# Feed-forward four slots behind attention, with its weights staged elsewhere and its two input projections in each other's banks

## What is computed

```
xn  = layernorm(x)
q   = xn @ Wq.T;  lat = xn @ Wkv_down.T;  k = lat @ Wk_up.T;  v = lat @ Wv_up.T
att = softmax(q k^T / 8) v @ Wo.T
xq  = fp4(xn)                        # block scale = max|x| / 6, nearest grid value
h   = silu(xq @ fp4(w_gate).T) * (xq @ fp4(w_up).T)
out = x + att + fp4(h) @ fp4(w_down).T
```

## Time and profile before

| | |
|---|---|
| median of 3 runs | 1498.85 us (1498.58 to 1499.34) |
| profiled execution | 1497.88 us |
| its span, first to last instruction | 1496.1 us |
| mean granted TensorE clock | 0.984 |
| TensorE busy | 1383.9 us (93%) |
| GpSimd busy | 1213.7 us (81%) |
| VectorE busy | 1189.6 us (80%) |
| ScalarE busy | 716.9 us (48%) |

### The profile page before, as it was taken

The page is one execution under the profiler, slowest core; times in us unless marked ns, Lnnn a source line. Parts: engine busy times, 40 slices in busy tenths (PEclk is TensorE's granted clock), DMA queues, the critical chain, the costliest instruction groups (busy, mean ns, idle before and its releaser), DMA issues.

```text
span 1496.1 us, 25492 instructions
## 1 busy us (share of the span) xinstructions
PE 1383.9 (93%) x7910; PEld 1021.1 (68%) x7910; DVE 1189.6 (80%) x2472; ACT 716.9 (48%) x1574; POOL 1213.7 (81%) x1336
## 2 busy tenths in 40 slices
PE   1489999999999999999999999999999999999996
PEld 1356677776767777676777677677767767676675
DVE  7677978888787888878888887888888788867662
ACT  3444545445454544545454454545454554545441
POOL 7648888879788887978888788879878887986773
PEclk9689999999999999999999999999999999999998
DMA  4032222222223222222222222222212322221220
GB/s 125 0 78 56 62 79 69 61 65 71 72 58 78 71 65 58 72 75 60 72 72 67 55 72 79 64 65 72 74 50 70 82 63 62 65 68 49 59 58 29
DMA packets 73557, 98.07 MB, mean 66 GB/s; under 512 B 12752, under 2 KB 40144, under 8 KB 73424
## 3 DMA queue, kind: packets, MB, share of 16 engines
q1 hardware_dynamic: 73424, 96.45, 24.4%
HBM read 37.16 MB, written 8.65 MB: 31 GB/s over the span
## 4 chain that ended last, share of the span: by engine, by line
PE 63%; DVE 17%; POOL 11%; issue 4%; ACT 3%; DMA 1%; SPq 0%; POOLq 0%; DVEq 0%; ACTq 0%
PE m L871 30%; PE po L1032 12%; PE mx L971 5%; PE st L999 5%; PE st L1000 5%; POOL key_sum L518 4%; DVE row_max L723 4%; PE m L1046 2%; DVE inv_den L794 2%; DVE hid L768 2%; DVE hid L764 2%; DVE xn L819 1%; PE m L1124 1%; PE m L983 1%; POOL h_norm L537 1%
## 5 line engine op out<-in xcount | busy, mean ns | idle before, releaser
L608 ACT ACTIVATE probs<-st 128x512 f32<-128x512 f32 x512 | 284.0, 594 | 334.3 <-PE st L1000 334.3
L518 POOL TENSOR_TENSOR key_sum<-key_sum,probs 128x512 f32<-128x512 f32 x256 | 329.1, 1285 | 38.0 <-ACT probs L608 1.7
L723 DVE TENSOR_REDUCE row_max<-mx 128x1 f32<-128x512 f32 x512 | 322.9, 672 | 1.2 <-PE mx L971 0.6
L1032 PE MATMUL po<-probs,lat_tok 128*64 128x512 f32 x1024 | 233.8, 598 | 0.0
L999 PE MATMUL st<-q_hi,lat 128*128 128x512 f32 x512 | 216.9, 424 | 0.5 <-ACT probs L608 0.5
L1000 PE MATMUL st<-q_lo,lat 65*128 65x512 f32 x512 | 203.1, 397 | 0.0
L971 PE MATMUL mx<-lat,q_hi 128*128 128x512 f32 x512 | 176.0, 418 | 11.4 <-DVE row_max L723 4.3
L871 PE MATMUL m<-wgu_hi,xt_hi 128*128 128x352 f32 x512 | 168.8, 330 | 3.5 <-DVE lat_tok L851 1.7
L616 ACT ACTIVATE hid<-m 128x352 f32<-128x352 f32 x128 | 59.5, 465 | 233.7 <-PE m L871 233.7
L871 PE MATMUL m<-wgu_hi,xt_lo 128*128 128x352 f32 x512 | 166.3, 325 | 0.0
L871 PE MATMUL m<-wgu_lo,xt_hi 128*128 128x352 f32 x512 | 166.1, 324 | 0.0
(11 more groups left out here) (179 smaller groups left out, 3347.4 us busy)
## 6 DMA issues: line engine op xcount, KB each, us to landing
q_hi<-qp_hi SPq DMA_DIRECT2D x256, 128.0 KB, 2.3
q_lo<-qp_lo SPq DMA_DIRECT2D x128, 128.0 KB, 2.4
inv_b<-inv_rows SPq DMA_DIRECT2D x128, 128.0 KB, 2.8
x_in<-in_L_attn_x_dram SPq DMA_DIRECT2D x64, 128.0 KB, 2.3
acc<-in_L_attn_x_dram SPq DMA_DIRECT2D x64, 128.0 KB, 2.1
out_dram<-acc SPq DMA_DIRECT2D x32, 256.0 KB, 2.9
q_lo<-neg_max SPq DMA_DIRECT2D x128, 2.0 KB
inv_rows<-inv_den SPq DMA_DIRECT2D x64, 4.0 KB
```

The lines of the kernel that those rows point to most:

```text
L518: pool.tensor_tensor(total, first, last, ALU.add).then_inc(sum_step, 1)
L608: act.activation(probs[:, t.c % 2, kc, :], st[kc % 2][:, :], ACT.Exp).then_inc(exp_done, 1)
L723: dve.tensor_reduce(row_max[:, u.c % 2, qc:qc + 1], mx[qc % 2][:, :], AX.X, ALU.max).then_inc(mx_taken, 1)
L1032: last = pe.matmul(po[v * R:(v + 1) * R, :], lat_tok[:, s.c % 2, kc, 0:R], probs[:, v, kc, :], start=(kc == 0), stop=(kc == CH - 1))
```

## The change

The feed-forward part of slot t now works on what slot t - 4 worked on (`ffn(t)`, `LAG = 4`), on every engine: gate, up, tanh, `hid`, scales, quantisation, transposes and down products. Slots 0 to 3 hold attention alone, and `TAIL` is nine slots, of which the first four hold feed-forward without attention. The late weight jobs are spread, one at the start and one in the middle of each slot from -4 to 2, all through bank m0, each waiting for both halves of the one before. Their staging moves: gate and down weights lie under the buffers that follow `hq` (`ht_hi`, `ht_lo` and others), which slot 6 writes first, and the second working buffer of quantisation is now part of `hq`. The wait for all jobs stands ahead of slot 4.

Gate now goes to m1 and up to m0. The query product and the latents therefore wait for `silu_done`, down products and the output projection for `hid_done`. Gate goes first except behind latents and their transposes (slots 5 and 7), where up does; before, up went first in slots 3 and 4 of a sequence.

In the residual buffer `acc` the output projection is now added before three of the four down products, so waits between the two kinds of sum are exchanged, and the store of a half waits for both and is issued in slots 4 and 8 of the following sequence, instead of 3 and 4.

```diff
+    LAG = 4
-        with nc.sbuf_tensor("weights_in", [P, 3 * CH * T], F32) as stage:
+        with nc.sbuf_tensor("weights_in", [P, 2 * PAIRS * P + PAIRS * D], F32) as stage:
...
+        with nc.sbuf_tensor("ffn_in", [P, -(-I // P) * D + KD * I], F32) as ffn_stage:
+            fflat = ffn_stage[:, :]
...
+        def ffn(t):
+            return t.plus(-LAG)
...
         def down_chunk(t):
-            n = t.plus(-5).over(2)
+            n = ffn(t).plus(-5).over(2)
+        def stored_half(t):
+            m = t.plus(-12).over(4)
+            return m if t.c % 4 == 0 and m.within(B * 2) else None
...
-        LEAD = [At(c) for c in range(-14, 0)]
-        TAIL = [At(SLOTS + c) for c in range(6)]
+        LEAD = [At(c) for c in range(-14, LAG)]
+        TAIL = [At(SLOTS + c) for c in range(LAG + 5)]
...
+        def lead_jobs(t, half):
+            if t.c == -5:
+                return range(len(EARLY)) if half == 0 else range(0)
+            n = len(EARLY) + 2 * (t.c + 4) + half
+            return range(n, n + 1) if t.c >= -4 and n < len(JOBS) else range(0)
+        def bank_of(n):
+            return WBANKS[n % 4] if n < len(EARLY) else m0
...
-                m = wov_half(t.plus(-1))
+                m = stored_half(t)
                 if m is not None:
-                    if t.i is None:
-                        sp.wait_ge(out_done, m.n(1, 1))
+                    sp.wait_ge(out_done, m.n(1, 1))
+                    sp.wait_ge(down_taken, m.n(2, 2))
...
-                d = t.over(2)
+                d = t.plus(-LAG).over(2)
...
-                    act.activation(hid[:, t.c % 2, :], m0[:, 0:HALF], ACT.Tanh, scale=0.5).then_inc(tanh_done, 1)
+                    act.activation(hid[:, f.c % 2, :], m1[:, 0:HALF], ACT.Tanh, scale=0.5).then_inc(tanh_done, 1)
...
                     dve.wait_ge(down_psum, d.n(1, 1))
+                    if d.c % CH:
+                        dve.wait_ge(out_done, d.over(CH).n(2, 1 + (d.c % CH) // 2))
...
                     dve.wait_ge(wov_psum, m.n(1, 1))
-                    dve.wait_ge(down_taken, m.n(2, 2))
+                    for c in range(2):
+                        dve.wait_ge(res_loaded[2 * j + c], s.n(16, 16))
+                    if j == 0:
+                        dve.wait_ge(down_taken, s.n(CH, 1))
...
+                    free = n if n >= len(EARLY) else n - 3
+                    if free > 0:
+                        pe.wait_ge(w_hi_done, free)
+                        pe.wait_ge(w_lo_done, LOWS[free])
...
             def gate(t):
+                if ffn(t).within(SLOTS):
+                    m1_free(t.plus(-1))
+                    into_hidden(ffn(t), m1, 0, gate_psum)
+            def up(t):
+                if ffn(t).within(SLOTS):
                     m0_free(t.plus(-1))
+                    into_hidden(ffn(t), m0, I, up_psum)
...
-                if wov_half(t.plus(-1)) is None:
+                if lat_seq(t.plus(-1)) is None and ltok_seq(t.plus(-1)) is None:
                     gate(t)
                     up(t)
...
                 if q_pair(t) is not None:
-                    if t.within(SLOTS):
-                        pe.wait_ge(hid_done, t.n(1, 1))
+                    if ffn(t).within(SLOTS):
+                        pe.wait_ge(silu_done, ffn(t).n(1, 1))
...
+                jobs(lead_jobs(t, 1))
                 query_scores(t, 2)
```

More of the change, by code:

```diff
@@ L493, in weights @@
             def weights(t, half):
-                for q in lead_work(t)[0][half:half + 1]:
+                for q in lead_quants(t)[half:half + 1]:
                     w, rows, cols = WQUANT[q]
@@ L682, in _ @@
                 weights(t, 0)
[L683 removed]
+                jobs(lead_jobs(t, 0))
                 slot(t)
@@ L759, in slot @@
                 max_rows(t, 1)
-                if t.within(SLOTS):
-                    h = hid[:, t.c % 2, :]
-                    dve.wait_ge(tanh_done, t.n(1, 1))
-                    dve.scalar_tensor_tensor(h, h, 1.0, m0[:, 0:HALF], ALU.add, ALU.mult).then_inc(silu_done, 1)
-                if t.within(SLOTS):
-                    dve.wait_ge(up_psum, t.n(1, 1))
-                    dve.wait_ge(silu_done, t.n(1, 1))
-                    dve.tensor_tensor(h, h, m1[:, 0:HALF], ALU.mult).then_inc(hid_done, 1)
-                u = t.plus(-2)
+                f = ffn(t)
+                if f.within(SLOTS):
+                    h = hid[:, f.c % 2, :]
+                    dve.wait_ge(tanh_done, f.n(1, 1))
+                    dve.scalar_tensor_tensor(h, h, 1.0, m1[:, 0:HALF], ALU.add, ALU.mult).then_inc(silu_done, 1)
+                if f.within(SLOTS):
+                    dve.wait_ge(up_psum, f.n(1, 1))
+                    dve.wait_ge(silu_done, f.n(1, 1))
+                    dve.tensor_tensor(h, h, m0[:, 0:HALF], ALU.mult).then_inc(hid_done, 1)
+                u = f.plus(-2)
                 if u.within(SLOTS):
@@ L928, in m0_free @@
                     pe.wait_ge(down_taken, down_chunk(t).n(1, 1))
-                elif t.within(SLOTS):
-                    pe.wait_ge(silu_done, t.n(1, 1))
+                elif ffn(t).within(SLOTS):
+                    pe.wait_ge(hid_done, ffn(t).n(1, 1))
             def m1_free(t):
@@ L1039, in weights_sum @@
                 if m is not None:
-                    if t.plus(-2).within(SLOTS) or t.plus(1).within(SLOTS):
+                    if ffn(t).plus(-2).within(SLOTS) or t.plus(1).within(SLOTS):
                         turned_taken(t)
```

105 lines of the change are left out of this document (48 added, 57 removed).

## The result

The changed kernel takes 1482.29 us (median of 4 runs, 1481.52 to 1483.24) against 1498.95 (1498.58 to 1499.34): a ratio of 0.9891, 95% interval 0.9877 to 0.9904. Its profiled execution took 1483.24, its span is 1481.4, the mean clock 0.986. 1482 was forecast.

What follows compares the result with a forecast made beforehand. TensorE was taken to bound the middle, GpSimd and VectorE not far behind. From 1496.1, -12.4 (beginning), -17 (middle) and +13 (end) gave a span of 1479.7; 1.8 and 1.0 added made 1482, range 1468 to 1496.

Steps and rivals of the forecast that it cites:

- The middle: Sequences 1 to 15: the bank swap saves 1.15 us per sequence, 17 us in all, bounds 9 to 27.
- Slot 3: Slot 3 of a sequence: with gate first, the query product's whole gap of 1.00 us goes; 0.95 taken.
- Slots 5 and 7: Slots after latents and their transposes: up then gate makes silu later; gain zero, between -0.1 and +0.2 us each.
- Slot 1 and its cap in slot 2: Query product 0.57 us earlier in slot 1, but GpSimd's key sums in slot 2 leave 0.26 free; 0.2 taken.
- Rival (a): Middle: the chain through VectorE and GpSimd takes the swap's gain; middle only -3, time 1496; chance 0.13.
- (b): More than forecast: slot 1's gain in full, middle -25, end only +8, time 1468; chance 0.15.
- (d): Middle: silu is the bound in slots 1 and 3 too, swap gains 0, time 1499; chance 0.06.
- The beginning: Up to slot 8: earlier start and lighter slots 0 to 7 save 12.4 us, bounds -16 to -6.
- 6 short jobs: Late weight jobs added to slots 0 to 3, which were still to take 26.6 us together, 8.8 less.
- early slots stay at 9 us: Beginning: a named sign that the forecast is wrong; slot 1 was put at 6.7 us, slot 2 at 8.2.
- The end: After the last key sum: four more feed-forward rounds, 4.5 us for shared m0, 1 for clock; +13, bounds +6 to +20.
- Rival (c): Both ends at 1.2 GHz: beginning -4, four unoverlapped end rounds of 12 us, +38; time 1516; chance 0.09.

## Why the prediction was right, and where not

**The middle** was right by its steps, with one of them in part unexplained. Slot 3: the whole gap went, 1.09 where 0.95 was taken. The prediction reckoned this gain from the order (gate first, so silu starts early) together with the wait for `silu_done`; with the wait undone slot 3 keeps it, so the order alone makes it. Slots 5 and 7: 0.60 from start to start, where 0.59 was worked out for slot 5, and 0.03 in all of slots 4 to 7 where 0 was taken; the shorter wait is what makes the late gate free there. Slot 1 and its cap in slot 2: the gap fell by 0.52 (0.57 worked out), the denominator product handed 0.26 back (0.31 worked out), and 0.21 stayed where 0.2 was taken. The denominator product's wait for the key sums appeared, as said, and GpSimd's part in it is shown by leaving out one of its operations. But with the wait undone slots 0 to 2 come out at 32.20, shorter still, so that 0.2 is not shown to come from the wait, and its fit is partly luck. The meetings of GpSimd with the small tensor_scalar, held at zero, took less of VectorE in the changed kernel (the tensor_scalars of the hidden block scales take 6.8 us in a sequence, where they took 8.1). Rival (a), a chain that takes what the swap gives, is out as a whole and true for slots 0 to 2; (b), slot 1 in full and a cheap end, is out by both its parts; (d) is out.

**The beginning** gave 9.7 and not 12.4; the sign was right and the size off. Slot 0 started at 91.08 (90.8 forecast). Slots 0 to 3 took 28.1 where 26.6 was summed: the term that was mis-sized is "6 short jobs", put at next to nothing. With the jobs ahead of slot 0 the four slots take 26.57, so they cost 1.5. That 26.57 meets the forecast sum is luck in part: slot 0 was shorter (4.20 for 4.9, which was reckoned at half clock; its clock was 0.70), slots 2 and 3 longer (8.30 for 8.2, 7.43 for 6.8). In the changed kernel slot 2 took 9.35, so the sign "early slots stay at 9 us" came up for one slot of the four. Slots 4 to 7 took 41.5 where 40.6 was forecast, because slot 4 lasted 12.2. TensorE's clock decides this: of the ten profiles of kernels with this beginning slot 4 takes 12.2 in the four where its mean granted clock was 0.86, and 10.7 to 10.8 in the six where it was 1.00. TensorE idled 1.34 to 1.36 ahead of that slot in all ten, so that gap alone does not tell which it will be. It is 1.5 us, and the prediction's lower bound of -6 had named such a clock.

**The end** gave 41.4 from the last key sum, 40 forecast. By steps: the first round 4.84 (4.7 forecast), the one with `on_lo` 6.58 (4.7 + 2.3), the last two 15.4 together (2 x 4.7 + 4.5 = 13.9), from the last `hq` to the end 10.8 (9.4 and 1 for the clock). The term that was mis-sized is the clock, put at 1: in this profile it is 2.9, in others up to 5. With the gaps filled the stretch takes 38.5, where the forecast without its 1 for the clock comes to 38.8, and the last two rounds take 14.05 for 13.9. The stall was named in the right place, the output projection standing between the last gate and up, but for one of its two links only: the path by `ht_hi` on ScalarE, which holds back `h_magic`, was missed, and that the 4.5 covered both is luck. Rival (c), rounds of 12 without overlap, is out; one round of 8.65 came near.

So the total is partly luck: the errors nearly cancelled, +2.7 at the beginning, -2.8 in the middle (19.8 for 17 over 15 sequences, the last one put at 1.3 like the others), +1.8 at the end (13.5 + 1.3 for 13). The span is 1481.4 where 1479.7 was summed. The prediction added 1.8 and 1.0 to get to the median (1482.5, written as 1482); this execution lies 0.9 above the median and not 1.0 below it, and that took the remaining 1.7 away again. The accounts named the halves' shares but drew no conclusion from them: -17 for the swap, +0.6 for the lag. By the runs the swap alone gives 22 to 23 us, and the lag as it was written costs 4 to 6. With the order in its end put right it is 1.5 to 2 ahead of the swap alone, whose end was left as it was.

## What to carry to other kernels

When an engine's queue is full over part of a period, a stall removed on another engine there is handed back within a slot or two: read gaps over the whole stretch between two slack places, not slot by slot. When work is shifted to the end of a kernel, write the in-order queues of the last rounds down by hand, since an order that was hidden under other work becomes the critical path, and each engine's order has to be turned, not TensorE's alone. Try the parts of a change alone: here one half carried it and the other cost. And when an operation is cut to test a link, look in the trace whether the time saved comes past the next meeting of two engines; if it does not, the run has tested nothing behind it.

## What the runs showed of the hardware

Before its two low stretches in the end TensorE had idled for 3.44 and 4.30 us. Full-rate matmuls of 128x256 then started 0.21 apart instead of 0.12. The first seven matmuls after the first gap still ran at the full rate. With identical code the low stretch after the second gap ended within the first down product in one profile and went on far into the second in another (0.73 over 4 us against 0.50 over 8 us above). The Trainium skill, "TensorE: Matmul & The Clock Gate", section "What's actually happening", says that the clock is throttled by default and that activity releases it; by that rule, the traces agree, since 58 matmuls without a purpose kept it at 1.00 and shortened the kernel.

A 128x1 power on GpSimd (`rstd`, L572) takes 0.55 us, as much as two thirds of a 128x352 multiply (0.79). So in a full queue an operation on very little data is not a cheap one.

The tensor_scalar on 128x22 of the block scales takes 0.17 to 0.18 us by itself. In the changed kernel's profile 94 took over 0.4 us, and every one of the 94 ended within 0.05 us of the end of a GpSimd instruction; in the kernel before it was 100 of 100.
